# A Mamba-style scan with a routed expert layer: three of sixteen state sums moved from VectorE to ScalarE and GpSimd, and a rearranged end

## The chip, the cores and the metric

The kernel runs on one core of a Trainium2 chip. Its time is the device time in microseconds (us) from launch to the last store. The kernel before took 1439.51 us (median of three runs, 1438.04 to 1442.42).

Engines are named as the profile names them: PE is the matrix engine, DVE the vector engine, ACT the scalar (activation) engine, POOL is GpSimd, and SP issues most of the transfers. Every engine works through its own list of instructions strictly in order and waits on semaphores.

## What is computed

All numbers are fp32. There are 32 sequences of 256 tokens with 128 features.

```python
x = x + mamba(layernorm(x), ...)
x = x + moe(layernorm(x), ...)

# mamba: 256 channels, 16 states for each channel
h = conv1d(xc, conv_w) + conv_b; u = h.T
dt = clip(sigmoid(u @ dt_w.T + dt_b), 1e-4, 1.0)
dA = exp(clip(dt * A)); dB = dt * B * u
state = dA * state + dB + 1e-6             # over time
y = sum over the 16 states of state * C, + D * u
y = (y * silu(z)) @ out_w.T

# moe: 8 experts of 256 hidden units, the best two for each token, and a shared one
shared = silu(x @ sg.T) * (x @ su.T) @ sd.T
routed = w0 * expert_a(x) + w1 * expert_b(x)
out = shared + routed
```

## The kernel before

**Groups and states.** The tokens are cut into 16 groups of 512 (two sequences). For each group the 16 states are taken one after another, so a *unit* is one state of one group, and there are 256. One unit passes through four engines:

1. ACT computes the decays `dA` (`decays`, L727 to L741) and for 5 of the 16 states also the inputs `dBT` by token (`state_input`, L784); POOL computes `dBT` for the other 11 (L621). `KINDS` says which.
2. PE transposes `dBT` into the two banks `p_db`, one for each half of the channels (`inputs_by_channel`, L854, names `i0`, `i1`).
3. DVE scans over time, `h <- dA, p_db`, one instruction for each half (L1070, names `s0`, `s1`).
4. PE transposes `h` back into `p_hT`, two banks (`states_by_token`, L866, name `h`), and DVE multiplies by C and adds to `yT` (`sum_states`, L1073, names `y0`, `y1`): four instructions of 128x256. For state 0 they are plain products (L1086), for the others product and sum (L1088).

`p_db` and `p_hT` exist once: PE can't write the next state before DVE has read the one there. `h` and `yT` exist twice.

**Around the states.** While the states of group g run, PE also computes group g+1's convolution, dt, B, C and z (names `xnT`, `u0`, `u1`, `dt0`, `dt1`, `bc`, `z0`, `z1`, `wT0`, `wT1`), all through one bank `p_misc`. For group g-1 come the transposes of `yT` (`yb0`, `yb1`), the skip term on DVE (`yd0`, `yd1`, L1101), the gate on POOL (L651), the output projection (`op`), the residual (`x1`, L1095), the second layer norm, and the router.

**Experts.** Two groups form a routed batch, and the last two groups are batches of their own. DVE sorts the tokens by expert in 29 small steps (`route`, L1112), the last of which writes `expert_of` (L1193). POOL scatters the rows to DRAM by indirect transfers (L665). Then come quads of four 128-row tiles: SP loads each tile's expert weights (384 KB) into a ring of eight (L514), PE computes gate, up and down (`G`, `U`, `N`), ACT the silu, DVE the product (`P`, L1199). POOL gathers the two results of each token back (L679), and DVE adds them, weighted, in eight instructions for a group (`add_routed`, L1206, name `C`). Every quad uses the same two banks `p_gu`, so its gate waits for the product of the quad before.

**What sets the order.** Tables of names, one line for each of the 16 units of a group (`PE_SLOTS`, `DVE_SLOTS`, `ACT_SLOTS`, `POOL_SLOTS`, `SP_SLOTS`), say in which order an engine does what; a line is called a slot here. `x` is a decay, `d` a state input, `c` a clamp, `S` scatters and gathers. `plan()` gives each piece of the expert layer a slot number, and lags from it. Nothing is reordered at run time.

## Time and profile before

| | before |
|---|---|
| median of 3 runs | 1439.51 us |
| profiled execution | 1441.34 us, span 1439.6 us |
| PE busy | 1240.6 us, 86% |
| DVE busy | 1221.1 us, 85% |
| ACT busy | 893.8 us, 62% |
| POOL busy | 791.7 us, 55% |
| chain that ended last | DVE 38%, PE 33%, issue 13%, ACT 9%, POOL 4% |

The span falls into three parts. Until 44.9 us constants and weights are loaded, and the first group is prepared. From 44.9 us, when the first scan starts, to about 1304 us the 256 units run. After that the last group's output, its router, and the remaining expert tiles follow, until 1439.6 us. In the middle part PE and DVE are both busy about nine tenths of the time, so a share of the span alone doesn't tell which of them sets the pace at a given place; the prediction reads stretches of one group instead.

### The profile page before, as it was taken

The page shows a single profiled execution, that of the slowest core. Times are in us where ns is not written, and L with a number is a line of the kernel's source. Part 1 is how long each engine was busy: PE and PEld are TensorE (multiplying, and loading weights), DVE is VectorE, ACT ScalarE, POOL GpSimd, SP SyncE. Part 2 cuts the span into 40 slices and gives each one's busy share as a digit, 9 for nine tenths or more (in the row PEclk, how much of TensorE's full clock was granted, in tenths as well). Part 3 has the DMA queues.
Part 4 walks back from the last instruction along what each step waited for, and adds up shares of the span by engine and source line. Part 5 has one row for each costly group of instructions (what it writes and reads, how often), then busy time and mean ns, then how long its engine had stood idle before and what let it go on. Part 6 is the DMA issues. An engine that isn't in the chain of part 4 may idle for free.

```text
span 1439.6 us, 27184 instructions
## 1 busy us (share of the span) xinstructions
PE 1240.6 (86%) x8709; PEld 1023.9 (71%) x8709; DVE 1221.1 (85%) x2396; ACT 893.8 (62%) x1399; POOL 791.7 (55%) x1318
## 2 busy tenths in 40 slices
PE   6788897899889898998989898998989898887883
PEld 3566666587777787786768777777777677776873
DVE  0699999898898989899998989999898989995331
ACT  2774757476776766666865766766765757752221
POOL 3445453854377553856467553866557553773342
PEclk9799999999999999999999999999999999998997
DMA  5000000032324143133423142133324142246873
GB/s 173 1 1 8 2 8 5 30 115 63 107 84 127 39 127 114 54 98 96 118 80 125 39 133 90 59 118 96 118 71 132 34 132 63 77 144 184 263 234 114
DMA packets 110655, 132.30 MB, mean 92 GB/s; under 512 B 10032, under 2 KB 81584, under 8 KB 110384
## 3 DMA queue, kind: packets, MB, share of 16 engines
q1 hardware_dynamic: 102320, 113.73, 25.6%
q0 software_dynamic: 8192, 16.79, 4.0%
q8 instruction: 73, 1.20, 0.3%
q14 instruction: 70, 0.57, 0.1%
HBM read 102.37 MB, written 28.11 MB: 91 GB/s over the span
## 4 chain that ended last, share of the span: by engine, by line
DVE 38%; PE 33%; issue 13%; ACT 9%; POOL 4%; DMA 2%; DVEq 0%; SPq 0%; POOLq 0%; ACTq 0%
DVE h L1070 17%; DVE yT L1088 12%; PE p_misc L908 6%; PE p_hT L876 5%; PE p_db L862 4%; PE p_dn L1015 4%; PE p_gu L1003 3%; PE p_misc L919 3%; ACT dA L740 2%; PE p_misc L902 2%; PE p_gu L995 2%; PE p_misc L945 1%; DVE x L1216 1%; POOL ysel L679 1%; POOL xs_dram L665 1%
## 5 line engine op out<-in xcount | busy, mean ns | idle before, releaser
L1070 DVE TENSOR_TENSOR_SCAN h<-dA,p_db 128x512 f32<-128x512 f32 x512 | 598.8, 1203 | 76.4 <-PE p_db L862 49.0
L632 POOL TENSOR_SCALAR dBT<-wT,bcT 128x256 f32<-128x256 f32 x704 | 338.6, 481 | 373.0 <-ACT wT L769 204.8
L1088 DVE SCALAR_TENSOR_TENSOR yT<-p_hT,bcT,yT 128x256 f32<-128x256 f32 x960 | 396.9, 471 | 9.4 <-PE p_hT L876 9.4
L862 PE MATMUL p_db<-ident,dBT 128*128 128x128 f32 x2048 | 297.3, 278 | 82.8 <-DVE h L1070 70.0
L862 PEld LDWEIGHTS p_db<-ident,dBT 128*128 128x128 f32 x2048 | 233.8, 142 | 145.6 <-issue 121.3
L740 ACT ACTIVATE dA<-dt_sb,A_sb 128x510 f32<-128x510 f32 x512 | 329.7, 709 | 5.4 <-DVE h L1070 4.7
L876 PE MATMUL p_hT<-ident,h 128*128 128x128 f32 x2048 | 292.7, 280 | 25.7 <-DVE yT L1088 16.5
L876 PEld LDWEIGHTS p_hT<-ident,h 128*128 128x128 f32 x2048 | 231.6, 143 | 68.4 <-DVE yT L1088 36.6
L679 POOL DMA_INDIRECT ysel<-ys_dram,slot x128 | 123.4, 964 | 97.3 <-DVE x L1216 38.4
L795 ACT ACTIVATE dBT<-wT,eps,bcT 128x256 f32<-128x256 f32 x320 | 163.5, 587 | 7.6 <-PE p_db L862 7.6
L665 POOL DMA_INDIRECT xs_dram<-xn,slot x128 | 126.8, 990 | 56.6 <-issue 36.0
L1199 DVE TENSOR_TENSOR hm<-p_gu,hm 128x512 f32<-128x512 f32 (+1 forms) x132 | 87.0, 663 | 71.7 <-PE p_gu L1003 70.6
L812 ACT ACTIVATE hm<-p_gu 128x512 f32<-128x512 f32 (+1 forms) x132 | 72.1, 581 | 109.3 <-PE p_gu L995 106.5
L1015 PE MATMUL p_dn<-wring,hm 128*128 128x128 f32 x764 | 106.3, 287 | 12.5 <-DVE hm L1199 12.5
L908 PE MATMUL p_misc<-xnT,wtap 128*128 128x512 f32 x256 | 116.1, 595 | 0.8 <-ACT u_sb L751 0.8
L1015 PEld LDWEIGHTS p_dn<-wring,hm 128*128 128x128 f32 x764 | 97.3, 201 | 15.4 <-DVE hm L1199 5.8
L1003 PE MATMUL p_gu<-xT,wring 128*128 128x128 f32 x764 | 105.6, 286 | 1.2 <-ACT hm L812 1.2
L1003 PEld LDWEIGHTS p_gu<-xT,wring 128*128 128x128 f32 x764 | 99.0, 202 | 10.1 <-issue 8.2
L995 PE MATMUL p_gu<-xT,wring 128*128 128x128 f32 x764 | 100.7, 276 | 6.0 <-issue 5.7
L751 ACT ACTIVATE u_sb<-p_misc,chan_sb 128x512 f32<-128x512 f32 x32 | 21.8, 680 | 127.8 <-PE p_misc L908 127.8
L995 PEld LDWEIGHTS p_gu<-xT,wring 128*128 128x128 f32 x764 | 93.2, 192 | 10.0 <-issue 7.7
L812 ACT ACT_TABLE_LOAD x53 | 68.0, 1283 | 34.1 <-PE p_gu L995 33.6
(115 smaller groups left out, 1374.3 us busy)
## 6 DMA issues: line engine op xcount, KB each, us to landing
wring<-w_moe_dram SPq DMA_DIRECT2D x191, 384.0 KB, 4.3
xt<-xs_dram SPq DMA_DIRECT2D x41, 256.0 KB, 4.8
ys_dram<-yo SPq DMA_DIRECT2D x41, 256.0 KB, 2.3
x_sb<-x_dram SPq DMA_DIRECT2D x16, 256.0 KB, 4.3
out_dram<-x SPq DMA_DIRECT2D x16, 256.0 KB, 2.6
xs_dram<-ysel SPq DMA_DIRECT2D x4, 512.0 KB, 5.5
xs_dram<-xn,slot POOLq DMA_INDIRECT x128, 2.3
ysel<-ys_dram,slot POOLq DMA_INDIRECT x128
```

Source lines behind the costliest of these rows:

```text
L632: op = pool.tensor_scalar(dBT[:, j % DBT_RING, c], wT[:, g % 2, c], bcT[:, g % 2, c, n:n + 1], STATE_EPS, ALU.mult, ALU.add)
L665: pool.indirect_dma_start(out=xs[b % 2], out_offset=bass.IndirectOffsetOnAxis(ap=slot[:, b % ROUTE_RING, j, c:c + 1], axis=0), in_=xn2[:, ...
L740: act.activation(dst[:, :, 1:], src[:, :, 1:], ACT.Exp, scale=A_sb[:, half, n:n + 1]).then_inc(exp_done, 1)
L795: op = act.activation(dBT[:, j % DBT_RING, c], wT[:, g % 2, c], ACT.Identity, scale=bcT[:, g % 2, c, n:n + 1], bias=eps[:])
L862: mm = pe.transpose(p_db[half][:, c * P:(c + 1) * P], dBT[:, j % DBT_RING, c, half * P:(half + 1) * P], ident[:])
L876: mm = pe.transpose(p_hT[pair][:, c, half * P:(half + 1) * P], h[:, j % 2, half, t0:t0 + P], ident[:])
L908: mm = pe.matmul(p_misc[:].rearrange("p (s t) -> p s t", s=SPG), wtap[:, t, half * P:(half + 1) * P], xnT[:, :, t:t + SEQ], start=t == 0, ...
L995: mm = pe.matmul(p_gu[i][:, half, cols], w[:, half * P:(half + 1) * P], tokens, start=True, stop=True)
L1003: mm = pe.matmul(p_gu[i][:, half, cols], w[:, HID + half * P:HID + (half + 1) * P], tokens, start=True, stop=True)
L1015: mm = pe.matmul(p_dn[:, t], hm[:, i, half, t % 2 * P:(t % 2 + 1) * P], w[:, 2 * HID + half * DM:2 * HID + (half + 1) * DM], start=half == ...
L1070: dve.tensor_tensor_scan(h[:, j % 2, half], dA[:, j % DA_RING, half], p_db[half][:], 0.0, ALU.mult, ALU.add).then_inc(scan_done, 1)
L1088: op = dve.scalar_tensor_tensor(yT[:, g % 2, cc], p_hT[pair][:, c], scalar, yT[:, g % 2, cc], ALU.mult, ALU.add)
```

## The change

- **The sums of states 0, 1 and 2 of each group leave DVE.** ACT multiplies the transposed state by C (`multiply_state`, names `m0`, `m1`): state 0 into `yT`, states 1 and 2 into a new buffer `y_more` that exists once. POOL adds `y_more` to `yT` (`add_more`). DVE's sum of state 3 waits for POOL's last addition. PE's transposes of a state wait for `mul_done` where ACT reads the one before.
- **The routed rows of groups 0 to 11 are added by POOL**: one product of 128x1024 and two additions of 128x512 (`add_routed` on POOL). DVE keeps groups 12 to 15.
- **At the end there are three sets of banks for the quads** (`p_gu`, `p_db`, `p_hT`, with `hm` and the two halves of `wT` as their buffers), and eight more places for expert weights in `dA`, free once the last scan is done. Quads come one slot apart from slot 257, two apart from slot 236.
- **New order tables**, with decays four units ahead in place of three, clamps two in place of one, rings of five in place of three for the router's results. The last three batches scatter two chunks in a slot.

The core of the diff:

```diff
+BY_ACT = 3
+COMB_DVE = 4
-CLAMP_LEAD = 1
-EXP_LEAD = 3
+CLAMP_LEAD = 2
+EXP_LEAD = 4
-ROUTE_RING = 3
+ROUTE_RING = 5
 DVE_SLOTS = (
-    "stats1 s0 s1 y0 y1", "P Q s0 C s1 y0 y1 yd0 P Q", "s0 s1 yd1 Q y0 y1 C", "s0 s1 C y0 y1 C P Q P",
+    "s0 s1 y0 y1", "stats1 P s0 s1 y0 C y1 Q yd0 P Q s0 Q", "s1 yd1 y0 y1 C", "C s0 s1 y0 y1 P C Q P",
...
-LAST_SCATTER = 6
+LAST_SCATTER = 3
-FAST_SLOTS = 12
-FAST_FROM = NS * GROUPS - FAST_SLOTS
-FAST_QUAD = 2
+TAIL = NS * GROUPS + 1
+TAIL_QUAD = 1
+TAIL_WEIGHT = 3
+END_SLOTS = 20
+END_FROM = NS * GROUPS - END_SLOTS
+END_QUAD = 2
-WEIGHT_LEAD = 2
+WEIGHT_LEAD = 1
+def bank_sets():
+    sets, before, last = [], [], {}
+    for at, (slot, _) in enumerate(ORDER):
+        chosen = 0 if slot < TAIL else (sets[-1] + 1) % 3
...
+        gu_banks = [p_gu, [p_db[i][:].rearrange("p (f t) -> p f t", f=2) for i in range(2)], p_hT]
+        hm_of = [hm[:]] + [wT[:, j].rearrange("p (i f) t -> p i f t", f=2) for j in range(2)]
...
+            def add_more(g, n, pair):
+                if g is None:
+                    return
+                pool.wait_ge(mul_done, sums_before(NS * g + n, pair, True))
+                at_least(pool, more_added, PAIRS * ((BY_ACT - 1) * g + n - 2) + pair + 1 if n > 1 else 0)
+                chunks = slice(2 * pair, 2 * pair + 2)
+                pool.tensor_tensor(yT[:, g % 2, chunks], yT[:, g % 2, chunks], y_more[:, chunks], ALU.add
+                                   ).then_inc(more_added, 1)
...
+            def add_routed(g, j):
+                b, m = place_of(g)
+                if j == 0:
+                    pool.wait_ge(ysel_loaded, 128 * (g + 1))
+                    pool.wait_ge(dn_emptied, QUAD["shared", g] + 1)
+                    shares = weight[:, b % ROUTE_RING, :, CHUNKS * m:CHUNKS * (m + 1)]
+                    pool.tensor_tensor(ysel[:], ysel[:], shares.rearrange("p j (c o) -> p j c o", o=1).broadcast_to(
+                        [P, 2, CHUNKS, DM]), ALU.mult).then_inc(comb_scaled, 1)
+                    pool.wait_ge(comb_scaled, g + 1)
+                else:
+                    pool.wait_ge(comb_done, 2 * g + 1)
+                pool.tensor_tensor(x1[:, g % X1_RING], x1[:, g % X1_RING], ysel[:, j], ALU.add).then_inc(comb_done, 1)
...
+            def multiply_state(g, n, pair):
+                j = NS * g + n
+                act.wait_ge(hT_in_psum, PAIRS * j + pair + 1)
...
+                for c in range(2):
+                    cc = 2 * pair + c
+                    into = yT[:, g % 2, cc] if n == 0 else y_more[:, cc]
+                    op = act.activation(into, p_hT[pair][:, c], ACT.Copy, scale=bcT[:, g % 2, cc, NS + n:NS + n + 1])
+                op.then_inc(mul_done, 1)
...
                 g, n = divmod(j, NS)
+                if n < BY_ACT:
+                    return
                 dve.wait_ge(hT_in_psum, PAIRS * j + pair + 1)
+                if n == BY_ACT == 1:
+                    dve.wait_ge(mul_done, sums_before(j - 1, pair, True))
+                elif n == BY_ACT:
+                    dve.wait_ge(more_added, PAIRS * ((BY_ACT - 1) * (g + 1) - 1) + pair + 1)
```

**ACT at the start of a group.** The decays of states 4 and on (`dA`), the inputs of states 3 and 4 (`dBT` x8), a quad's silu (`hm`), and the transposed input (`xnT`). Before:

```order
L740 ACTIVATE dA<-dt_sb,A_sb 128x2x255 x6
L795 ACTIVATE dBT<-wT,eps,bcT 128x256 x8
L740 ACTIVATE dA<-dt_sb,A_sb 128x2x255 x2
L812 ACT_TABLE_LOAD
L812 ACTIVATE hm<-p_gu 128x512
L812 ACTIVATE hm<-p_gu 128x2x128
L747 ACTIVATE xnT<-p_misc 128x2x256
L820 ACTIVATE yo<-p_dn 128x512
L740 ACT_TABLE_LOAD
L740 ACTIVATE dA<-dt_sb,A_sb 128x2x255 x2
L795 ACTIVATE dBT<-wT,eps,bcT 128x256 x4
```

The same place of the changed kernel:

```order
L835 ACTIVATE dA<-dt_sb,A_sb 128x2x255 x6
L891 ACTIVATE dBT<-wT,eps,bcT 128x256 x8
L911 ACTIVATE yT<-p_hT,bcT 128x256 x4
L835 ACTIVATE dA<-dt_sb,A_sb 128x2x255 x2
L931 ACT_TABLE_LOAD
L931 ACTIVATE hm<-p_gu 128x512
L931 ACTIVATE hm<-p_gu 128x2x128
L842 ACTIVATE xnT<-p_misc 128x2x256
L911 ACTIVATE y_more<-p_hT,bcT 128x256 x4
L939 ACTIVATE yo<-p_dn 128x512
L891 ACTIVATE dBT<-wT,eps,bcT 128x256 x4
L835 ACT_TABLE_LOAD
```

The three groups of four products (the third follows two rows later) stand between work that was there before; nothing was taken away between them.

**DVE at the start of a group.** `stats` is the first layer norm of the next group, `h` the scans, `yz` the skip term, `hm` the product of a quad. Before, from just ahead of state 0's scans to state 3's:

```order
L1047 BN_STATS stats<-x_sb 128x6 x4
L1050 BN_AGGR mv<-stats 128x2 x4
L1070 SCALAR_TENSOR_TENSOR h<-dA,p_db 128x512 x2
L1088 SCALAR_TENSOR_TENSOR yT<-p_hT,bcT,yT 128x256 x4
L1199 TENSOR_TENSOR hm<-p_gu,hm 128x512
L1070 SCALAR_TENSOR_TENSOR h<-dA,p_db 128x512 x2
L1086 TENSOR_SCALAR yT<-p_hT,bcT 128x256 x4
L1101 SCALAR_TENSOR_TENSOR yz<-u_sb,chan_sb,p_misc 128x512
L1070 SCALAR_TENSOR_TENSOR h<-dA,p_db 128x512 x2
L1101 SCALAR_TENSOR_TENSOR yz<-u_sb,chan_sb,p_misc 128x512
L1088 SCALAR_TENSOR_TENSOR yT<-p_hT,bcT,yT 128x256 x4
L1070 SCALAR_TENSOR_TENSOR h<-dA,p_db 128x512 x2
```

The same place of the changed kernel, on to state 4's scans:

```order
L1201 SCALAR_TENSOR_TENSOR h<-dA,p_db 128x512 x2
L1219 SCALAR_TENSOR_TENSOR yT<-p_hT,bcT,yT 128x256 x4
L1178 BN_STATS stats<-x_sb 128x6 x4
L1181 BN_AGGR mv<-stats 128x2 x4
L1332 TENSOR_TENSOR hm<-p_gu,hm 128x512
L1201 SCALAR_TENSOR_TENSOR h<-dA,p_db 128x512 x2
L1233 SCALAR_TENSOR_TENSOR yz<-u_sb,chan_sb,p_misc 128x512
L1201 SCALAR_TENSOR_TENSOR h<-dA,p_db 128x512 x2
L1233 SCALAR_TENSOR_TENSOR yz<-u_sb,chan_sb,p_misc 128x512
L1201 SCALAR_TENSOR_TENSOR h<-dA,p_db 128x512 x2
L1332 TENSOR_TENSOR hm<-p_gu,hm 128x512
L1201 SCALAR_TENSOR_TENSOR h<-dA,p_db 128x512
```

The statistics now follow state 0's scans, and no sum stands between the scans of states 1, 2 and 3. The sum that follows first is state 3's, between the two halves of state 4's scan.

**POOL at the start of a group whose batch is being scattered.** Changed kernel only: scatters (`xs_dram`), the layer norm (`rs`, `xn`), the gate (`yz`), and the additions.

```order
L635 TENSOR_TENSOR rs<-rs,neg_half 128x4
L638 TENSOR_SCALAR xn<-x_sb,nm,rs 128x128 x4
L726 TENSOR_TENSOR yz<-yz,sz 128x512
...
L740 DMA xs_dram<-xn,slot 2944x128 x2
L708 TENSOR_TENSOR yT<-yT,y_more 128x512 x2
L698 TENSOR_SCALAR dBT<-wT,bcT 128x256 x4
L740 DMA xs_dram<-xn,slot 2944x128 x2
...
L726 TENSOR_TENSOR yz<-yz,sz 128x512
L708 TENSOR_TENSOR yT<-yT,y_more 128x512 x2
```

The four additions stand behind scatters, a layer norm and both gates in the same queue.

## Rows read from the trace of the kernel before

**Rows 1.** The page's part 1: busy time, share, instructions.

```profile
PE 1240.6 (86%) x8709; PEld 1023.9 (71%) x8709; DVE 1221.1 (85%) x2396; ACT 893.8 (62%) x1399; POOL 791.7 (55%) x1318
```

**Rows 2.** Timeline of DVE (start, duration, instructions): state 0's sums, two groups apart.

```profile
658.87 1.63 DVE L1086 TENSOR_SCALAR yT<-p_hT,bcT 128x256 f32<-128x256 f32 x4
...
822.67 1.63 DVE L1086 TENSOR_SCALAR yT<-p_hT,bcT 128x256 f32<-128x256 f32 x4
```

**Rows 3.** Busy time by stretch: length, each engine (instructions), PE clock, DMA share, GB/s.

```profile
380.00:1180.00 800.00, 722.13 (x5235) 600.58 (x5234) 742.09 (x1446) 550.43 (x855) 484.15 (x773) 1.00 0.30 92
816.06:835.33 19.27, 17.59 (x116) 14.15 (x115) 17.73 (x30) 14.89 (x26) 15.87 (x24) 0.94 0.33 92
835.33:863.90 28.57, 27.42 (x199) 22.92 (x197) 25.22 (x52) 17.20 (x24) 14.03 (x28) 1.00 0.41 129
863.90:899.40 35.50, 30.67 (x253) 26.19 (x251) 34.07 (x76) 23.52 (x39) 12.49 (x21) 1.00 0.29 88
```

**Rows 4.** Timeline of DVE around the start of the group at 816 us.

```profile
811.25 2.31 DVE L1216 SCALAR_TENSOR_TENSOR x<-ysel,weight,x 128x128 f32<-128x128 f32 x8
...
814.86 0.87 DVE L1047 BATCH_NORM_STATS2 stats<-x_sb 128x6 f32<-128x128 f32 x4
...
816.06 2.30 DVE L1070 TENSOR_TENSOR_SCAN h<-dA,p_db 128x512 f32<-128x512 f32 x2
...
837.57 1.63 DVE L1088 SCALAR_TENSOR_TENSOR yT<-p_hT,bcT,yT 128x256 f32<-128x256 f32 x4
```

**Rows 5.** Timeline of PE: transposes of state 3 and of state 4.

```profile
836.20 1.04 PE L876 MATMUL p_hT<-ident,h 128*128 128x128 f32 x8
...
841.60 1.04 PE L876 MATMUL p_hT<-ident,h 128*128 128x128 f32 x8
```

**Rows 6.** Timeline of ACT in the same group (last number in brackets: idle before).

```profile
817.41 4.03 ACT L795 ACTIVATE dBT<-wT,eps,bcT 128x256 f32<-128x256 f32 x8
821.35 1.31 ACT L740 ACTIVATE dA<-dt_sb,A_sb 128x510 f32<-128x510 f32 x2
824.49 1.28 ACT L812 ACT_TABLE_LOAD   x1 [1.82 <-PE p_gu L995]
...
851.98 1.09 ACT L812 ACTIVATE hm<-p_gu 128x512 f32<-128x512 f32 x2
```

**Rows 7.** Groups of instructions by line (busy, mean ns | idle before, releaser).

```profile
L764 ACT ACTIVATE bcT<-p_misc 128x128 f32<-128x128 f32 x16 | 4.3, 266 | 14.4 <-PE p_misc L945 14.4
...
L651 POOL TENSOR_TENSOR yz<-yz,sz 128x512 f32<-128x512 f32 x32 | 40.9, 1278 | 34.5 <-DVE yz L1101 34.3
```

**Rows 8.** Timeline of POOL: a layer norm's ends, the inputs ahead of a batch's scatters.

```profile
843.13 0.20 POOL L566 TENSOR_SCALAR rs<-mv 128x4 f32<-128x4 f32 x1 [5.33 <-DVE mv L1050]
...
844.87 1.74 POOL L572 TENSOR_SCALAR xn<-x,nm,rs 128x128 f32<-128x128 f32 x4
...
891.82 4.38 POOL L632 TENSOR_SCALAR dBT<-wT,bcT 128x256 f32<-128x256 f32 x8 [18.45 <-ACT wT L769]
```

**Rows 9.** Timelines of POOL and DVE at one moment of the router.

```profile
870.87 2.50 POOL L646 TENSOR_TENSOR w_sb<-dt_sb,u_sb 128x512 f32<-128x512 f32 x2
```

```profile
872.30 1.15 DVE L1140 TENSOR_TENSOR key<-rest,top 128x64 f32<-128x64 f32 x1
```

**Rows 10.** Timeline of the end, DVE: the last scans, the last router step.

```profile
1301.60 2.31 DVE L1070 TENSOR_TENSOR_SCAN h<-dA,p_db 128x512 f32<-128x512 f32 x2
...
1347.01 0.17 DVE L1193 TENSOR_SCALAR expert_of<-expert_f 1x15 int32<-1x15 f32 x1
```

**Rows 11.** Timeline of the end, POOL: gathers of groups 12, 13 and 15.

```profile
1360.51 0.99 POOL L679 DMA_INDIRECT ysel<-ys_dram,slot  x1 [3.19 <-issue]
...
1377.81 0.95 POOL L679 DMA_INDIRECT ysel<-ys_dram,slot  x1 [7.49 <-DVE x L1216]
...
1423.09 0.95 POOL L679 DMA_INDIRECT ysel<-ys_dram,slot  x1 [18.77 <-DMA ys_dram<-yo]
...
1431.88 0.95 POOL L679 DMA_INDIRECT ysel<-ys_dram,slot  x1 [0.30 <-issue]
```

More of the change, by code:

```diff
@@ L34 @@
 DT_MIN = 1e-4
-BATCHES = tuple((g, g + 1) for g in range(0, GROUPS - 2, 2)) + ((GROUPS - 2,), (GROUPS - 1,))
+ALONE = 2
+BATCHES = tuple((g, g + 1) for g in range(0, GROUPS - ALONE, 2)) + tuple((g,) for g in range(GROUPS - ALONE, GROUPS))
 MOST = max(len(gs) for gs in BATCHES) * CHUNKS
@@ L177 @@
 QUAD = {quad: at for at, (_, quad) in enumerate(ORDER)}
+def bank_sets():
+    sets, before, last = [], [], {}
+    for at, (slot, _) in enumerate(ORDER):
+        chosen = 0 if slot < TAIL else (sets[-1] + 1) % 3
+        sets.append(chosen)
+        before.append(last.get(chosen))
+        last[chosen] = at
+    return sets, before
+BANK_SET, BEFORE = bank_sets()
 def tiles_of_quad(quad):
@@ L217, in plan @@
         slot = max(ended[b] + GATHER_LAG, last_gather)
-        per = 1 if ended[b] < FAST_FROM else 4
+        per = 1 if ended[b] < TAIL else 4
         for g in gs:
@@ L296, in routed_quad, with sums_before @@
     return b, at - XT0[b]
+def sums_before(j, pair, by_act):
+    if j < 0:
+        return 0
+    full, n = divmod(j, NS)
+    if by_act:
+        return PAIRS * (full * BY_ACT + min(n, BY_ACT)) + (pair + 1 if n < BY_ACT else 0)
+    return PAIRS * (full * (NS - BY_ACT) + max(0, n - BY_ACT)) + (pair + 1 if n >= BY_ACT else 0)
 def of_kind(kind, j):
@@ L450, in build @@
         mac_done = sem("mac_done")
+        mul_done = sem("mul_done")
+        more_added = sem("more_added")
         yz_ready = sem("yz_ready")
@@ L461, in build @@
         w_loaded = [sem(f"w_loaded{j}") for j in range(W_RING)]
+        spare_loaded = [sem(f"spare_loaded{j}") for j in range(SPARE)]
         gate_in_psum = sem("gate_in_psum")
@@ L704, in _ @@
                         weigh_u(ahead, int(name[1]))
+                    if name in ("m0", "m1") and u - NS * k < BY_ACT - 1:
+                        add_more(group_of(k, 0), u - NS * k + 1, int(name[1]))
                     if name in ("gate0", "gate1") and behind is not None:
                         gate(behind, int(name[4]))
+                    if name == "C":
+                        for g, j in due.get(("comb", u), ()):
+                            if g < GROUPS - COMB_DVE:
+                                add_routed(g, j)
                     if name == "S":
@@ L807, in silu @@
                 at = QUAD[quad]
-                at_least(act, down_in_psum, at)
+                into, banks = hm_of[BANK_SET[at]], gu_banks[BANK_SET[at]]
+                if BEFORE[at] is not None:
+                    act.wait_ge(down_in_psum, BEFORE[at] + 1)
+                elif BANK_SET[at]:
+                    act.wait_ge(scan_done, HALVES * UNITS)
                 for i in range(2):
@@ L811, in silu @@
                     act.wait_ge(gate_in_psum, 2 * at + i + 1)
-                    act.activation(hm[:, i, :, 0:n], p_gu[i][:, :, 0:n], ACT.Silu).then_inc(silu_done, 1)
+                    act.activation(into[:, i, :, 0:n], banks[i][:, :, 0:n], ACT.Silu).then_inc(silu_done, 1)
             def empty_down(b, q):
@@ L827, in _ @@
                         state_input(u + DB_LEAD)
+                    if name in ("m0", "m1") and u - NS * k < BY_ACT:
+                        multiply_state(group_of(k, 0), u - NS * k, int(name[1]))
                     if name in MISC_STAGE and group_of(k, MISC_STAGE[name]) is not None:
@@ L871, in states_by_token @@
                 for pair in range(PAIRS):
-                    at_least(pe, mac_done, PAIRS * (j - 1) + pair + 1)
+                    if j and (j - 1) % NS < BY_ACT:
+                        pe.wait_ge(mul_done, sums_before(j - 1, pair, True))
+                    elif j:
+                        pe.wait_ge(mac_done, sums_before(j - 1, pair, False))
                     for c in range(2):
```

140 lines of the change are left out of this document (87 added, 53 removed), and 28 rows, old and new, of tables (ACT_SLOTS, DVE_LAST, DVE_SLOTS, PE_SLOTS).

## Prediction

> **What bounds the kernel now.** I read the busy shares first: PE 86%, DVE 85%, ACT 62%, POOL 55% [rows 1]. They name two candidates and settle nothing. In the timeline of DVE the reader looks for a landmark that comes once in a group, state 0's sums. They are 163.8 us apart over two groups (658.87 to 822.67), so 81.9 us for a group [rows 2]. Over 800 us of that, PE is busy 722.1 and DVE 742.1, which makes 73.9 and 76.0 us in a group, with 8.0 and 5.9 us idle [rows 3]. Neither can be the bound alone; the next view has to say where each one is.
>
> I cut the group that starts at 816.06 us into three stretches [rows 3].
> - A, the scans of states 0 to 3: 19.3 us, PE busy 17.6, DVE 17.7.
> - B, states 4 to 8, where the convolution, dt and B, C of the next group lie on PE: 28.6 us, PE busy 27.4, DVE 25.2. PE sets the pace.
> - C, states 9 to 15: 35.5 us, DVE busy 34.1, PE 30.7. DVE sets the pace.
>
> The sums that the change takes from DVE all lie in A. B is PE's and C keeps all its own. That is the main reading: what is removed is large, and where it is removed, something else is nearly as late.
>
> **Stretch C and its edge: what comes off.** Four sums take 1.63 us [rows 2]; end to end that is 0.39 each, so twelve make 4.7 us for a group. They are in A. In C two things go. The statistics of the next layer norm stood ahead of state 0's scans and now follow them: from 814.86 to 816.06, 1.2 us for every group [rows 4]. The eight routed additions, 2.3 us [rows 4], are in C in one group of two; in the other they lie in B, under PE, and I count them at nothing. That gives 1.2 + 2.3/2 = 2.35 us for a group.
>
> **Stretch A: what takes the sums' place.** The path was scan, transposes, sum on DVE. It is now scan, transposes, product on ACT, addition on POOL, sum of state 3 on DVE. I follow ACT's list from the start of state 0's scans (time 0). The third pair of decays waits for those scans, 2.3 us [rows 4], and takes 1.3, so 3.6. Eight state inputs take 4.0 [rows 6]: 7.6. Then come state 0's four products.
>
> No row shows such a product (128x256 from a PSUM bank, with a scale for each partition). From below, a plain copy of 128x128 from PSUM takes 0.27 us [rows 7]; from above, a state input of the same size, with scale and bias, is 4.03/8 = 0.50 end to end [rows 6]. The nearest is the state input, less its bias. I take 0.40, so 1.6 for a state; the ends give 1.1 and 2.0.
>
> Onward: 9.2 after state 0; decays 1.3, 10.5; table load 1.3 and two silus 1.1 [rows 6], 12.9; the transposed input 0.5, 13.4; state 1's products, 15.0; a state input 2.0 and an output of a quad 0.6, 17.6; table load and decays 2.6, 20.2; state 2's products, 21.8. Before, PE finished transposing state 3 at about 837.1, 21.0 us after the start [rows 5]. Now these transposes wait for state 2's products and end near 22.5, because nothing was taken out of ACT's list between them.
>
> POOL is second in the path. A two-input operation of 128x512 takes 1.28 us [rows 7], so the four additions are 5.1 us for a group, on an engine that is busy 15.9 of 19.3 us in A [rows 3]. A batch's scatters can begin when the next states' inputs are out, at 896.2 [rows 8]; that is 4.4 us before the next group's time 0, which is 1.2 us of statistics behind the end of C. Up to the last addition the new order has ten scatters (1.26 each, as the gathers, 1423.09 to 1431.88 for seven [rows 11]), two state inputs (2.2 each), a layer norm (3.5) [rows 8], two gates (2.6) and the four additions (5.1): 28.2 us. I get the last addition out at 24 to 25, so state 3's sums end near 27, where they ended at 839.2 (23.1) before [rows 4]. PE's transposes of state 4 were reached at 841.60, 25.5 us after the start [rows 5], because PE was late anyhow. So 2.4 us of the delay are hidden and 1 to 1.5 us are not. I take a loss of 1.0 us for a group; from zero, if ACT and POOL run ahead of this, up to 5.1, if one more block of routed additions stands in front.
>
> Main part: 2.35 - 1.0 = 1.35 us for each of 13 groups with expert work, 17.6 us. For the first three I take nothing: they have no quads, and the 2.3 us of decays and the state inputs stand before the products just as well.
>
> **Two rules of the Trainium skill.** The router step at 872.30 took 1.15 us, while POOL's products of two SBUF inputs ran from 870.87 to 873.37; it ended with them [rows 9]. The sums, of which one input is a PSUM bank, take 1.63 us for four in every row here [rows 2, 4]. The Trainium skill (SBUF — State Buffer, "Who interferes with whom") says that a DVE instruction with two SBUF inputs and a GpSimd instruction that reads SBUF exclude each other, and that one with at most one SBUF input doesn't contend. The trace agrees. By that rule the additions cost DVE nothing. It speaks against the change in one place: the two products `w0` and `w1` now stand in two slots of the router, and each may stop a step for some 0.9 us, 8 us in all over eight routed batches.
>
> For ACT's product the Trainium skill (ScalarE: Activation LUTs, "What ACT_TABLE_LOAD costs") gives 280 ns and 0.833 ns for each element, an estimate of 0.49 us for 256 elements. The trace's end-to-end times are below its figure. With 0.49 state 2's products would be out 1.1 us later, and the main part would save about 14 us less.
>
> **The end.** Time from the last scan to the last router step, 1303.9 to 1347.2: 43.3 us [rows 10]. In it stand 2.3 us of routed additions and waits for quads behind one another; with more banks and group 11's rows on POOL I take 3 us off. Then: eight scatters, 10.2 us; idle 3.2; four groups of eight gathers, 10.05 each; idle between them 7.5, about as much again, and 18.8; and 1432.83 to 1439.6 for the last landing, the additions and the store [rows 11]. The gathers need nothing from the banks but that batch 8's quads are done. The 18.8 us were that wait. With three sets of banks and sixteen places for weights it shrinks to what the others show, 7.5, and the 3.2 go to 0.5. That is 14 us, with the 3 us 17. POOL's list of 40 indirect transfers at 1.26 us then holds the end, and no bank helps further.
>
> The last group gets two more quads and scatters at double rate; I set this at nothing, within 4 us either way.
>
> **The sum.** 1441.3 (the profiled execution) - 17.6 - 17 = 1406.7. The median of the runs is 1.8 us lower, so 1405 us. The difference that a measurement can tell from none is 0.3%, 4.3 us.
>
> **Rivals.**
> 1. The sums come off in full, since the tables also move PE's work. For it: DVE has 5.9 us idle in a group, and half of PE's 8.0 may be DVE's doing. Against: A, where the sums are, has both engines at 17.7 of 19.3, and B is PE's. DVE loses 4.7 + 2.3 = 7.0 us; PE's 73.9 and 2 us of unavoidable gaps stop it at 76, so 5.9 x 13 + 4.7 x 3 = 91 us, and 17 at the end: 1332. Half of it: 1377.
> 2. Slower: the chain over ACT and POOL takes DVE's place. State 3's sum waits for POOL's fourth addition, and everything behind it waits too. If the loss in A is 5.1 us in place of 1.0 (one block of routed additions, 2.6 + 2 x 1.28, ahead of it), the main part costs 2.75 x 13 = 36 us more, less 17: 1458. It decides from a loss of 2.35 + 17/13 = 3.7 us on. For it: ACT's list is full there, and POOL's too. Against: before, 2.4 us were spare.
> 3. The end gives nothing, because the expert weights of batch 8 land no earlier (the wait of 18.8 us stays). Then the main part alone: 1439.5 - 17.6 = 1422.
>
> **How the numbers follow.** Forecast 50%, rival 1 in full or in part 25%, rival 2 13%, rival 3 12%. The forecast's own range is 1385 to 1425. For eight in ten I reach down past the half of rival 1, to 1362, and up to where rival 2 has just lost the whole gain, 1437. Faster by over 0.3%: the forecast, rivals 1 and 3, less some edge, 85%; within 0.3% 5%; slower 10%.
>
> **What would show it.** In the changed profile the landmark, now state 3's sums, should lie about 161 us apart for two groups (between 159 and 163); at 152 rival 1 is right, above 164 rival 2. DVE's busy time should fall by 16 x 4.7 + 12 x 2.3, about 100 us, much more than the span does. Its idle time before state 3's sums should name POOL's additions. ACT's products should have some 0.4 us end to end. At the end the idle time before group 15's gathers should be near 7 us. The forecast is wrong if stretch A is shorter than 18 us, or if PE waits for `mul_done` less than 0.5 us a group.

## The result: 3% slower, and the profile after

The changed kernel takes 1484.83 us (median of four runs, 1483.70 to 1484.93), the kernel before, beside it, 1438.78 (1437.89 to 1442.42). The ratio is 1.030, 95% interval 1.028 to 1.032. Forecast were 1405 us, within 1362 to 1437. It went the way of rival 2, with more than its price.

Busy times of the changed kernel's page stand against [rows 1]: DVE lost 83 us of work (forecast were about 100; part of the difference is in the router, see below), PE 7, ACT gained 70 and POOL 136. The span rose by 43.5.

```profile
PE 1233.4 (83%) x8709; PEld 1026.0 (69%) x8709; DVE 1138.5 (77%) x2108; ACT 963.9 (65%) x1592; POOL 927.7 (63%) x1418
```

The landmark is the first layer norm's statistics, once in a group, in DVE's timeline. Two groups of the changed kernel are 170.45 us apart, against 163.8 in [rows 2].

```profile
763.85 0.85 DVE L1178 BATCH_NORM_STATS2 stats<-x_sb 128x6 f32<-128x128 f32 x4
...
934.30 0.85 DVE L1178 BATCH_NORM_STATS2 stats<-x_sb 128x6 f32<-128x128 f32 x4
```

The same stretches as in [rows 3], of the changed kernel: 800 us, then A, B, C of a group, then A of the next.

```profile
380.00:1180.00 800.00, 697.17 (x5072) 586.50 (x5072) 665.46 (x1213) 572.90 (x933) 550.07 (x804) 0.99 0.29 87
...
840.02:864.22 24.20, 18.27 (x128) 14.63 (x128) 14.31 (x25) 21.23 (x41) 19.78 (x27) 1.00 0.68 204
864.22:893.53 29.31, 27.48 (x201) 23.18 (x201) 23.37 (x44) 17.55 (x25) 19.11 (x30) 1.00 0.28 84
893.53:930.50 36.97, 31.37 (x245) 28.04 (x244) 35.98 (x75) 24.99 (x40) 16.31 (x26) 0.91 0.22 65
930.50:952.50 22.00, 18.26 (x128) 14.62 (x128) 14.32 (x26) 20.89 (x41) 17.90 (x26) 1.00 0.34 103
```

A grew from 19.3 to 24.2 us. DVE is busy only 14.3 of them, PE 18.3: PE's idle time in A went from 1.7 to 5.9, DVE's from 1.5 to 9.9. Neither is the bound there; both wait for ACT and POOL, and for each other. B grew by 0.7 us (even groups) and 1.1 (odd ones); C grew by 0.2 in the even groups and fell by 3.4 in the odd ones. DVE's timeline shows where A is lost:

```profile
840.02 2.32 DVE L1201 TENSOR_TENSOR_SCAN h<-dA,p_db 128x512 f32<-128x512 f32 x2
...
848.45 2.33 DVE L1201 TENSOR_TENSOR_SCAN h<-dA,p_db 128x512 f32<-128x512 f32 x2
856.96 0.75 DVE L1233 SCALAR_TENSOR_TENSOR yz<-u_sb,chan_sb,p_misc 128x512 f32<-128x512 f32 x1 [6.18 <-PE p_misc L1011]
857.62 2.32 DVE L1201 TENSOR_TENSOR_SCAN h<-dA,p_db 128x512 f32<-128x512 f32 x2
863.62 0.69 DVE L1332 TENSOR_TENSOR hm<-p_gu,hm 128x512 f32<-128x512 f32 x1 [3.67 <-PE p_gu L1134]
864.22 1.21 DVE L1201 TENSOR_TENSOR_SCAN h<-dA,p_db 128x512 f32<-128x512 f32 x1
```

The first wait, 6.18 us, is for `yb1`, which the new PE table has behind `xnT`, the transposes of the normalized input. In the whole profile such waits are 75.9 us; before they were 1.3. ACT and POOL in the same moments:

```profile
847.54 1.53 ACT L911 ACTIVATE yT<-p_hT,bcT 128x256 f32<-128x256 f32 x4
...
855.12 0.60 ACT L931 ACTIVATE hm<-p_gu 128x512 f32<-128x512 f32 x1 [2.91 <-PE p_gu L1125]
855.62 0.59 ACT L842 ACTIVATE xnT<-p_misc 128x512 f32<-128x512 f32 x1
856.09 1.57 ACT L911 ACTIVATE y_more<-p_hT,bcT 128x256 f32<-128x256 f32 x4
...
862.65 1.55 ACT L911 ACTIVATE y_more<-p_hT,bcT 128x256 f32<-128x256 f32 x4
```

```profile
850.80 1.75 POOL L638 TENSOR_SCALAR xn<-x_sb,nm,rs 128x128 f32<-128x128 f32 x4
...
865.54 2.50 POOL L708 TENSOR_TENSOR yT<-yT,y_more 128x512 f32<-128x512 f32 x2
```

The loop is to be read here. POOL's layer norm is out at 852.55, 12.5 us after the start of A (before: 824.83, 8.8 us). PE's transposes of it start at 852.69, a gate matmul (L1125) stands behind them, ACT's silu waits for that gate and ends at 855.72, and state 1's products begin at 856.09, though PE had finished transposing that state at 851.3. Four products take 1.53 us, 0.38 each: the 0.40 taken was right.

PE's list shows how the delays pass on. Its waits between 400 and 1180 us add up to 68 us before and 97 in the changed kernel, about 3 us more for a group, which is what a group lost. None of these lines has a counterpart before:

```profile
PE p_misc L1011 <- ACT xnT L842: 9.5, 9, 1.2
PE p_misc L1011 <- DVE yT L1219: 9.0, 9, 1.0
...
PE p_misc L1021 <- POOL xn L638: 5.5, 4, 1.4
...
PE p_hT L1000 <- ACT y_more L911: 1.5, 9, 0.2
```

The last of them is the wait of the transposes for products themselves (`mul_done`), under 0.2 us for a group. The prediction had named less than 0.5 us there as a sign against itself. The products act through what stands behind them, and hardly through that wait.

Cut at the scans in DVE's timeline, the loss of 61.4 us up to the last scan (1301.60 before, 1362.98 after) is: first scan 4.1 later; groups 0 to 3, 1.9; groups 4 to 13, 30.7; groups 14 and 15, 24.7. Behind the last scan 17.9 us came back (138.0 before, 120.1 after). Windows of group 15 (A, B) and of the time behind the last scan, changed kernel:

```profile
1273.40:1305.00 31.60, 19.19 (x129) 17.59 (x128) 14.74 (x20) 23.78 (x44) 23.95 (x27) 0.89 0.36 111
1305.00:1327.20 22.20, 19.43 (x171) 18.43 (x170) 22.13 (x44) 10.51 (x15) 15.48 (x28) 1.00 0.33 108
...
1365.30:1483.10 117.80, 76.28 (x579) 70.75 (x577) 37.74 (x107) 25.21 (x47) 55.83 (x60) 0.89 0.59 187
```

The gathers of the last four groups in POOL's timeline, to be laid beside [rows 11]: the longest gap ahead of one is 9.0 us, where it was 18.8.

```profile
1432.60 0.94 POOL L754 DMA_INDIRECT ysel<-ys_dram,slot  x1 [5.72 <-DVE x L1350]
...
1451.28 0.94 POOL L754 DMA_INDIRECT ysel<-ys_dram,slot  x1 [9.01 <-DVE x L1350]
...
1466.49 0.94 POOL L754 DMA_INDIRECT ysel<-ys_dram,slot  x1 [5.51 <-DMA ys_dram<-yo]
```

### The profile page after: what moved, and what is told of

The parts are those of the page before. It is cut to its first block, busy times and chain, and to the rows that moved or that the text cites. A ratio compares the mean times of both kernels' runs of the same rounds, so it can differ in the third digit from the quotient of the medians.

```text
span 1483.1 us, 27197 instructions
## 1 busy us (share of the span) xinstructions
PE 1233.4 (83%) x8709; PEld 1026.0 (69%) x8709; DVE 1138.5 (77%) x2108; ACT 963.9 (65%) x1592; POOL 927.7 (63%) x1418
## 3 DMA queue, kind: packets, MB, share of 16 engines
q1 hardware_dynamic: 102320, 113.73, 24.7%
## 4 chain that ended last, share of the span: by engine, by line
PE 33%; DVE 23%; issue 15%; ACT 13%; POOL 13%; DMA 1%; SPq 1%; POOLq 0%; DVEq 0%; ACTq 0%
DVE h L1201 11%; DVE yT L1219 8%; PE p_db L983 5%; PE p_hT L1000 5%; PE p_dn L1146 4%; PE p_misc L1032 4%; POOL dBT L698 3%; ACT dA L835 3%; PE p_gu L1125 3%; PE p_gu L1134 3%; PE p_misc L1043 2%; POOL xs_dram L740 2%; POOL ysel L754 2%; PE p_misc L1026 2%; ACT dBT L891 2%
## 5 line engine op out<-in xcount | busy, mean ns | idle before, releaser
L1219 DVE SCALAR_TENSOR_TENSOR yT<-p_hT,bcT,yT 128x256 f32<-128x256 f32 x832 | 344.5, 470 | 29.8 <-PE p_hT L1000 15.3
L983 PE MATMUL p_db<-ident,dBT 128*128 128x128 f32 x2048 | 302.7, 280 | 75.0 <-DVE h L1201 64.9
L835 ACT ACTIVATE dA<-dt_sb,A_sb 128x510 f32<-128x510 f32 x512 | 332.5, 712 | 22.6 <-DVE h L1201 20.6
L983 PEld LDWEIGHTS p_db<-ident,dBT 128*128 128x128 f32 x2048 | 239.6, 144 | 138.7 <-issue 108.2
L1000 PEld LDWEIGHTS p_hT<-ident,h 128*128 128x128 f32 x2048 | 235.5, 144 | 66.4 <-issue 41.3
L740 POOL DMA_INDIRECT xs_dram<-xn,slot x128 | 127.3, 994 | 58.4 <-issue 34.3
L1332 DVE TENSOR_TENSOR hm<-p_gu,hm 128x512 f32<-128x512 f32 x118 | 77.6, 663 | 63.5 <-PE p_gu L1134 63.3
L931 ACT ACTIVATE hm<-p_gu 128x512 f32<-128x512 f32 x118 | 65.3, 584 | 72.9 <-PE p_gu L1125 67.9
L708 POOL TENSOR_TENSOR yT<-yT,y_more 128x512 f32<-128x512 f32 x64 | 80.0, 1271 | 29.8 <-ACT y_more L911 29.7
L1146 PE MATMUL p_dn<-wring,hm 128*128 128x128 f32 x664 | 91.4, 284 | 5.2 <-DVE hm L1332 4.2
L1125 PE MATMUL p_gu<-xT,wring 128*128 128x128 f32 x664 | 87.1, 277 | 2.4 <-ACT xT L877 1.2
L1134 PE MATMUL p_gu<-xT,wring 128*128 128x128 f32 x664 | 88.3, 278 | 0.3 <-ACT hm L931 0.3
L1146 PEld LDWEIGHTS p_dn<-wring,hm 128*128 128x128 f32 x664 | 83.8, 199 | 6.6 <-issue 2.5
L931 ACT ACT_TABLE_LOAD x54 | 69.3, 1283 | 24.8 <-PE p_gu L1125 21.9
```

Source lines behind the costliest of these rows:

```text
L740: pool.indirect_dma_start(out=xs[b % 2], out_offset=bass.IndirectOffsetOnAxis(ap=slot[:, b % ROUTE_RING, j, c:c + 1], axis=0), in_=xn2[:, ...
L835: act.activation(dst[:, :, 1:], src[:, :, 1:], ACT.Exp, scale=A_sb[:, half, n:n + 1]).then_inc(exp_done, 1)
L931: act.activation(into[:, i, :, 0:n], banks[i][:, :, 0:n], ACT.Silu).then_inc(silu_done, 1)
L983: mm = pe.transpose(p_db[half][:, c * P:(c + 1) * P], dBT[:, j % DBT_RING, c, half * P:(half + 1) * P], ident[:])
L1000: mm = pe.transpose(p_hT[pair][:, c, half * P:(half + 1) * P], h[:, j % 2, half, t0:t0 + P], ident[:])
L1146: mm = pe.matmul(p_dn[:, t], hm_of[BANK_SET[at]][:, i, half, t % 2 * P:(t % 2 + 1) * P], w[:, 2 * HID + half * DM:2 * HID + (half + 1) * D ...
```

## Experiments

The runs came in five groups, each on a chip of its own with runs of the kernel before beside it. That took 1465 us on four of these chips and 1441 on the fifth. Two steady groups of the changed kernel's lists take 170.2 to 170.4 us on four chips; with the lists of before they take 163.8 on the first chip and 164.1 to 164.9 on two others, so a difference of 1 us to before is no more than their scatter. The end differs more. So two numbers are given: the ratio to before on the same chip, and the length of two steady groups (start of group 6's scans to start of group 14's, over four, from DVE's timeline), with A of an even and an odd group. These are to be laid beside 163.8 (19.3, 19.0) before and 170.3 (24.2, 22.0) after.

**The changed kernel once more.** No edit.

> The changed kernel as it is, once more, beside the others of this group, since the end of the program takes another time from chip to chip. The steady groups should be those of its first profile to 0.1 us (stretch A 24.2 and 22.0 us, two groups 170.5); its ratio to the kernel before was 1.030 and is expected between 1.03 and 1.045.

1.0436 (1.041 to 1.046); two groups 170.4 us, A 24.2 and 22.0. The steady loss repeats. From the last scan to the end it takes 154.9 us here, 120.1 on the first chip. With the old lists (experiment 10, banks alone) that stretch takes 146.6 us on another of the chips with 1465 us: the gain of 17.9 us behind the last scan is seen on the first chip only.

**1. yb1 early.**

```
-    "h i0 i1 G U N", "h X xnT i0 i1 U N G yb1"
+    "h i0 i1 G U N yb1", "h X xnT i0 i1 U N G"
```

> One move in the changed kernel: PE transposes the second half of yT (yb1) at the end of slot 1, ahead of the layer norm's transposes (xnT), as in the kernel before, and not at the end of slot 2. Theory P (the place of yb1): DVE's 75.9 us of waits for this transpose are the loss, since the scan of state 3 is queued behind it. It expects stretch A (scan of state 0 to scan of state 4) to fall from 24.2 and 22.0 us to about 20 and the time to 1440 us, the gain of the tail (some 16 us) just paying the rest. Theory L (the lists of ACT and POOL): the transposes xnT wait for a late layer norm of POOL, the silu of ACT waits for the gate matmul behind xnT, the products m0, m1 stand behind that silu, and PE's transposes of h wait for the products. It expects that the wait of DVE only moves from yb1 to p_db or p_hT: A stays within 1 us of before, 1470 to 1485 us.

1.0444 (1.042 to 1.047), two groups 170.8, A 24.2 and 22.6. Waits of DVE between 400 and 1180 us, first in the changed kernel, then here:

```profile
DVE yz L1233 <- PE p_misc L1011: 44.6, 9, 6.2
DVE hm L1332 <- PE p_gu L1134: 36.2, 17, 3.7
DVE h L1201 <- PE p_db L983: 27.0, 27, 2.1
```

```profile
DVE hm L1332 <- PE p_gu L1134: 66.5, 17, 7.4
DVE h L1201 <- PE p_db L983: 36.8, 32, 2.2
...
DVE yz L1233 <- PE p_misc L1011: 1.5, 9, 0.3
```

43 us of one wait turned into 40 us of two others. The longest wait in the list was worth nothing by itself. Theory P falls, L stands so far.

**2. All sums back on DVE,** in the changed order (`BY_ACT = 0`).

> The changed kernel with its own order, but the sums of all sixteen states on DVE: no products on ACT, no additions of them on POOL. Theory L expects A to fall to 20 us in spite of 4.7 us more work of DVE in it, since PE waits no more for products and additions: 3 us in each of 13 groups, about 1445 us. Theory P expects A to stay at 22 to 24 (yb1 still stands behind xnT), or to grow by what DVE has to do behind it: 1485 to 1530 us. If the chain of products were harmless, the time must rise by up to 4.7 x 16 = 75 us.

1.054 (1.051 to 1.057), two groups 172.8, A 26.8 and 24.8. L's expectation did not come true: without the products A is longer still, as theory P had it. Neither theory holds in both runs.

**3. Both together.** The edit of 1 and that of 2.

> The changed kernel's order with all sums on DVE, as in the run before with sums on DVE, and yb1 ahead of xnT too, so that DVE's sum of state 1 no longer stands behind the wait for yb1. That run alone had A of 25.8 and 25.8 us, yb1 alone 24.2 and 22.6. If the two waits cover for each other, A falls to 21 to 22.5 us, two groups to 166 to 168. If only the late layer norm and the longer list of PE set A, it stays at 24 to 26.

1.0208 (1.018 to 1.023), two groups 166.3, A 22.8 and 22.1. The two waits cover for each other. With yb1 late the products cost nothing, and even save 2.5 us (170.3 with, 172.8 without); with yb1 early they cost 4.5 us (170.8 with, 166.3 without). Of the 6.5 us that two groups lost, 2.5 stay with the new order, in which the routed rows are still on POOL.

**4. One state's products.** As 3, with `BY_ACT = 1`: state 0 on ACT, nothing on POOL.

> The changed kernel with yb1 ahead of xnT and the product of state 0 alone on ACT. With no state on ACT two groups took 166.3 us, with three 170.7. If the cost goes with the number of products: 167.5 to 168. If it comes with the second and third (PE's transposes wait for products that stand behind the silu, state 3's sum for POOL): 165 to 166.5.

1.0172 (1.015 to 1.020), two groups 164.6, A 22.4 and 20.8, and so 1.7 us less than with none. It is the second and third state that cost: 6.2 us for two groups. Only they need `y_more`, a free place in it, and POOL's additions. No run separates ACT's eight further products from these additions.

**5. Products in the old lists.** The kernel before, with `BY_ACT = 3` and

```
-ACT  "x V E d d X",       "x V d xnT E",       "x V E X"
+ACT  "x m0 m1 V E d d X", "x m0 m1 V d xnT E", "m0 m1 x V E X"
-POOL "gate0 c d S c",       "S gate1 d c c"
+POOL "gate0 m0 m1 c d S c", "m0 m1 S gate1 d c c"
```

> The kernel before with one part of the change: the products of states 0 to 2 on ACT and two additions of each pair on POOL, put into the old lists where the sums' transposes are out (ACT slots 1 to 3 ahead of the silu, POOL slots 2 and 3). Everything else, the routed rows, the order of the rest and the end too, is that of before. Theory O (the new order of the lists, not the moved work, stretches A): A stays at 19.3 and 19.0 us or falls by up to 1 us, and the time is 0.990 to 1.003 of before. Theory M (the moved work itself, a chain of ACT and POOL in the recurrence): A grows to 21 to 23 us as in the changed kernel, 1.02 to 1.035.

1.0393 (1.036 to 1.042), two groups 172.1: M in kind, and more in the time than it said. But A, at 20.3 and 21.3, lies under or at the low end of M's range, and more was lost in B, which grew from 28.6 and 26.7 to 30.0 and 30.1. From PE's waits, 400 to 1180 us:

```profile
PE p_misc L1030 <- ACT xnT L840: 14.8, 9, 2.1
PE p_hT L998 <- DVE yT L1224: 13.4, 17, 1.9
PE p_misc L1024 <- POOL yz L724: 8.2, 5, 1.7
PE p_misc L1036 <- POOL xn L636: 7.4, 5, 1.5
```

The convolution waits for ACT's copy `xnT`, queued behind products; the output projection waits for POOL's gate, queued behind additions. The second layer norm's transposes wait for POOL too. None of the three waits of 14.8, 8.2 and 7.4 us is in PE's list of before, whose smallest entry is 0.3 us; the fourth is 11.7 there. In these lists the moved work costs by what is queued behind it.

**6. One state in the old lists.**

> The kernel before with the product of state 0 alone on ACT (in ACT's slot 1, ahead of the silu), nothing on POOL; DVE's sum of state 1 then adds to it. It tells ACT's share of the cost from POOL's. With three states on the old lists two groups took 172 to 173 us instead of 164.7. If every product costs on ACT's list (1.6 us in front of the state inputs and the silu, which PE waits for), one state costs about a third, 2.5 to 3 us in two groups, ratio 1.010 to 1.015. If the additions on POOL and the wait of DVE and PE for them are the cost, one state costs nothing or gains DVE's 1.6 us: two groups 162 to 165 us, 0.99 to 1.001.

0.998 (0.9963 to 0.9997), two groups 165.3, on another chip 164.9 with the lists of before. The only version under 1, by 0.2%: one state's products are free, and hardly a gain either. That DVE is not alone in setting A is the likely reason. Against 172.1 with three states, the second and third cost 6.8 us in two groups, much as the 6.2 in the new order.

**7. Routed rows, from both sides.** First the changed kernel with all rows on DVE (`COMB_DVE = 16`), then the kernel before with rows on POOL (`COMB_DVE = 4`, `C` in POOL's table).

> The changed kernel with the additions of the routed rows of all sixteen groups on DVE (COMB_DVE 16), so that POOL has 4.5 us less in each of twelve groups. Theory R (POOL's routed additions and gathers hold up the layer norm, and with it PE's transposes): A of the groups that follow such a block falls from 24.2 to about 22.0, 2.2 us in six groups, and DVE's 2.3 us for each group cost something in stretch C: 1475 to 1490 us. Without R nothing is won in A and DVE's 12 x 2.3 = 28 us come on top: 1500 to 1512 us.

> The kernel before with the routed rows of the first twelve groups added on POOL, in its old lists (POOL's additions at the slots of the changed kernel), and nothing else. In the changed order this was worth 0.9 us in two groups: 2.1 off stretch C of the odd groups, 1.2 more in A of the even ones. Expected from that: ratio 0.990 to 0.998. If POOL's 4.5 us hold up the layer norm in the old order more than DVE gains, 1.000 to 1.01.

1.0438 (1.041 to 1.047) with two groups at 171.2, and 1.0099 (1.008 to 1.012) with 166.9. In the changed order A of the even groups fell to 23.0, half of what theory R said, and C of the odd ones grew by 2.1: the rows on POOL are worth 0.9 us in two groups there, and the whole time does not show it. The second run missed its first range and came out in the second. In the old lists C of the odd groups is 2.2 us shorter (33.7 to 31.5), A of the even ones 4.8 longer (24.1). The 4.5 us of additions and the gathers stand ahead of state 2's input on POOL, and PE waits for it. PE's wait in A of group 10, then its windows before, during and after:

```profile
PE p_db L981 <- POOL dBT L696: 3.9, 1, 3.9
```

```profile
826.60:832.30 5.70, 1.72 (x12) 1.26 (x13) 5.69 (x10) 5.63 (x11) 4.73 (x7) 0.84 0.46 131
832.30:837.40 5.10, 5.10 (x24) 5.10 (x25) 2.33 (x2) 1.28 (x1) 4.61 (x9) 0.51 0.01 3
837.40:842.00 4.60, 4.56 (x42) 4.32 (x40) 3.95 (x7) 1.84 (x4) 3.68 (x4) 1.00 0.17 45
```

After 3.9 us idle PE goes on at a granted clock of 0.51, the level of 1.2 GHz, for 5 us, which costs another 2.5, an estimate from half the speed over these 5 us. Why the same rows are a gain of 0.9 in the changed kernel is not shown; that its chain of products is as late anyway would explain it.

**8. Both on the kernel before.**

> Both of these on the kernel before: routed rows on POOL and the product of state 0 on ACT. If the two save DVE's time independently, the sum of both differences; if each only uncovers PE, no more than the better one.

1.0066 (1.004 to 1.009). With 0.998 and 1.0099 alone, the sum would be 1.008, which lies in the interval; the better one alone does not. The two are independent within the noise.

**9. Four moves against PE's waits.** yb1 early (PE), `stats1` ahead of `s0` (DVE), `ln1` ahead of gathers (POOL), `m0 m1` ahead of `V` (ACT).

> The changed kernel with four moves that aim at PE's waits in A: yb1 back ahead of xnT (PE), the statistics of the layer norm back ahead of state 0's scans (DVE), the layer norm ahead of two gathers (POOL), state 1's products ahead of the silu that waits for a gate matmul behind xnT (ACT). PE was idle 5.9 and 3.7 us of A, before 1.7 and 2.6. Theory O: these waits are the loss, A falls by 2.5 to 4 us, two groups from 170.5 to 164 to 167 us, and the ratio to the changed kernel is 0.970 to 0.985. If the loss is not in these waits (theory M: PE's transposes of h wait for products and additions wherever they stand), two groups stay within 1.5 us of 170.5.

> The changed order with all sums on DVE and yb1 ahead of xnT (1.0208 of before, two groups 166.3 us, before 163.8), and besides the statistics of the layer norm back ahead of state 0's scans and the layer norm ahead of two gathers on POOL. Theory N (the remaining 2.5 us of two groups are the late layer norm): two groups 163.5 to 165 us, ratio 1.008 to 1.015. If they are PE's longer list in A (one more expert matmul block there), it stays within 0.7 us of 166.3.

1.0428 (1.040 to 1.045), two groups 170.7; and the same moves with the sums on DVE 1.0294 (1.026 to 1.033), 167.2. In the first, A fell to 20.9 in odd groups and stayed at 24.2 in even ones on average, and C got the 1.2 us of statistics back. The time is within what theory M said. With the sums on DVE A fell by 0.8 and 1.2, C grew by as much, and B of the odd groups by 0.6: theory N falls. The late layer norm is not the remaining cost; which of the new list's moves is stays open.

**10. The end.** The kernel before with the changed end; that with batch 6's scatters spread; the changed kernel with them spread; the kernel before with three sets of banks alone.

```
-    put("scatter", scatter_from(b) + c // chunks_per_slot(b), b, c)
+    put("scatter", scatter_from(b) + ((0, 1, 2, 3, 4, 4, 5, 5)[c] if b == 6 else c // chunks_per_slot(b)), b, c)
```

> The kernel before in its main part (its lists for the sixteen groups, its leads, all sums and all additions on DVE), with the end of the changed one: its lists for the last stages, three sets of banks and sixteen places for weights, the quads at double pace for the last twenty slots, two chunks of scatters in a slot from batch 6 on. From the last residual to the end the changed kernel takes 101.5 us, before 117.4: that expects 1439 - 16 = 1423 us. If the double rate of batch 6's scatters is what stretches group 15's A from 17.7 to 31.6 us, that group is longer here too, by 5 to 14 us, and the time is 1428 to 1437 us. If the tail's gain hangs on the additions that POOL took over, about 1439 us.

> The kernel before with the end of the changed one, as in the run with the tail alone (1.0167 of before; A of group 15 34.3 us), with the same spreading of batch 6's scatters. Theory S: A of group 15 falls from 34.3 to 20 to 25 us, the ratio from 1.0167 to 1.005 to 1.010. If the 16 us that the tail of the changed kernel saved in its first profile hold on this chip, it would be under 1.

> The changed kernel with one edit: the eight chunks of scatters of batch 6 are spread over six slots (0,1,2,3,4,4,5,5 behind the first) and not over four, while the quads keep their slots. Theory S (scatters at double rate stand on POOL ahead of the inputs of states 2 and 3 of group 15, and PE, ACT and DVE wait behind them): group 15's A, 34.5 us on the chip of the last runs and 31.6 in the first profile, falls to 22 to 27 us, and the time by 7 to 12 us. If the group waits for something else (the shared experts' quad, weights), A stays and the time is that of the changed kernel, 1.0436 of before, within 3 us.

> The kernel before with all its lists, rates and numbers, and only three sets of banks and the sixteen places for weights behind the last scan. Theory W (the resources themselves shorten the end): the waits of the gate matmuls for products and of the weight loads for free places go, 5 to 15 us less, ratio 0.990 to 0.997. Theory T (only the quicker pace of the changed lists uses them): within 3 us of before, 0.998 to 1.002.

1.0167 (1.014 to 1.020), 1.0141 (1.011 to 1.018), 1.0512 (1.048 to 1.055), 1.0001 (0.998 to 1.002). The banks and places alone are worth nothing: T. The changed end costs 25 us, and 22 with the scatters spread, where it was expected to save 16. Group 15's A is 34.3 us with the changed end, 19.1 with the old one. Spreading the scatters takes A to 28.6 in the one kernel and from 34.5 to 30.4 in the other, but B of the changed kernel rises from 24.0 to 41.6, as PE's transposes of the rows (`xt`) then wait up to 10.1 us for their transfer. Theory S is half right: the pile of scatters is a part. The doubled pace of quads inside the scans may be another; no run sets it alone.

**11. The old end in the new main part.**

> The changed kernel with the end of the kernel before: its lists for the last stages, two sets of banks and eight places for weights, double pace for the last twelve slots only, one chunk of scatters in a slot for batches 6 and 7. It separates the end's share of the loss from the steady groups'. On this chip the changed kernel is 1.0436 of before, 64 us. Steady groups 4 to 13: 30 us of that. Theory E (the new end costs on this chip, group 15's A 34.5 us against 19.1): A of group 15 is 21 to 24 us, the ratio 1.024 to 1.033. If the end gives its 16 us back as in the first profile, this run is slower than the changed kernel, 1.05.

> The best main part found in the new order (yb1 ahead of xnT, only state 0's product on ACT, routed rows on POOL; two groups 164.6 us, before 164.7) with the end of the kernel before. It starts its scans 4 us later, since POOL's clamps stand ahead of the first inputs, and its groups should be as long as those of before: ratio 1.000 to 1.005, against 1.0172 with the new end. Above 1.010 the end is not what costs there.

1.0658 (1.063 to 1.068) and 1.0373 (1.035 to 1.040): both misses. A of group 15 is indeed 17.2 and 16.6 us, and the last scan of the first starts at 1349.5, 13.5 us earlier than in the changed kernel on the first chip. But behind the last scan both take over 180 us, where before took 138. Both kept the weights' lead of one slot (`WEIGHT_LEAD = 1`, before 2), which is the likely reason: too short for eight places behind the scans. No run changes it alone. PE's largest wait behind 1350 us, in the first:

```profile
PE p_gu L1124 <- DMA wring<-w_moe_dram: 36.4, 10, 5.7
```

So they price the end's cost within the scans, 13.5 us, but not its gain behind them.

## Why the prediction was wrong

- **Stretch C and its edge:** 2.35 us for a group were forecast to come off. Measured (mean of even and odd) 1.6, all of it in the odd groups: 3.4 there, -0.2 in the even ones, where 1.2 were forecast. Right in kind, too large.
- **Stretch A, the failed step.** "2.4 us of the delay are hidden and 1 to 1.5 us are not": a loss of 1.0 was taken, measured are 3.9 (4.9 and 3.0), and 0.9 in B, which was put at nothing. I followed ACT's list as if only its own work filled it and wrote "table load 1.3 and two silus 1.1". The second silu waited 2.91 us for a gate matmul behind `xnT`; up to that wait the list ran as forecast (state 0's products were out at 9.1 us, 9.2 were forecast), and behind it everything was 2.4 to 2.6 us late. State 2's products ended 24.2 us after the start, not 21.8, PE's transposes of state 3 at 26.2, not 22.5, POOL's last addition at 28.0, not 24 to 25, and state 3's sums at 29.6, not 27. And the wait that I named (state 3's sum for POOL's fourth addition) is not where the time shows: DVE waits 6.6 us for it in the whole run. PE's list carries it, where `h` of the next state, `xnT`, `yb1` each wait a little and everything queued behind them moves. I had read the new PE table's `yb1`, but gave it no price. Experiment 9 moved state 1's products ahead of that silu, with three other moves, and two groups stayed at 170.7. So that one wait does not explain the loss by itself: what it gives back is lost elsewhere.

  A wait of the same kind was in the trace of before, where no product stood in the list. The second silu ended 13.4 us after the start there, not at the 12.9 of the forecast, though that had 1.6 us of products ahead of it:

```profile
828.89 0.60 ACT L812 ACTIVATE hm<-p_gu 128x512 f32<-128x512 f32 x1 [2.51 <-PE p_gu L995]
```

- **Rival 2** named the mechanism and its place, if not its size (1458 us against 1485). Its argument against, "before, 2.4 us were spare", held for one state's products (experiment 6), and not for three (experiment 5). State 3's sum waiting for POOL, its own step, is the small part.
- **Rival 1** assumed DVE or PE as the bound of A; PE is busy only 18.3 us of 24.2.
- **The start** was set at nothing: the first scan is 4.1 us later, since POOL's clamps, with a lead of two, wait for more decays ahead of its first inputs. POOL's first inputs start at 45.6 us, where they started at 36.5.
- **The last groups** were set at nothing, within 4 us. They took 24.7 more, of which 13.5 go with the new end by experiment 11, on another chip.
- **The end:** forecast 17 off, measured 17.9 behind the last scan on the first chip. Its parts came out near too: up to the last router step 2.0 off (forecast 3), behind it 15.9 (forecast 14), and the gap ahead of group 15's gathers 5.5 us (forecast 7.5). But the reason given, more banks, is not shown: alone they gave nothing. On the chips with 1465 us the stretch is not shorter at all (154.9 against 146.6). The number is in part luck.

Put into the sum: the main part without start and new end took 61.4 - 4.1 - 13.5 = 43.8 us more, forecast were 17.6 less, which makes a miss of 61.4 (by chance the same figure as the whole loss up to the last scan). So 1406.7 + 61.4 + 4.1 + 13.5 - 0.9 = 1484.8, against 1484.93 for the profiled execution. That the sum closes proves nothing, since its terms are read from the same runs. It says where the miss lies: some 18 us of the 78 are in the start and the new end, which I set at nothing, and most of the rest in A and B.

**The router beside POOL.** The router's steps at 903.88 and 904.78 took 0.86 and 1.19 us while POOL's products of two SBUF inputs ran from 903.39; the second of them takes 0.21 us without a partner (874.95 before).

```profile
903.39 2.50 POOL L721 TENSOR_TENSOR w_sb<-dt_sb,u_sb 128x512 f32<-128x512 f32 x2
```

```profile
903.88 0.86 DVE L1272 TENSOR_TENSOR key<-rest,top 128x64 f32<-128x64 f32 x1
904.78 1.19 DVE L1275 TENSOR_TENSOR key<-key,rank 128x64 f32<-128x64 f32 x1
```

This is what the Trainium skill (SBUF — State Buffer, "Who interferes with whom") says of a DVE instruction with two SBUF inputs beside a reading GpSimd; the trace agrees, 1.6 us for this batch. Before, one such step was stopped already (1.15 us, [rows 9]). Over the whole run the steps `key<-rest,top`, `key<-key,rank` and `rest<-hit,prob` of the seven batches of two groups took 7.4 us more than before, near the 8 us that the prediction gave. Its eight routed batches are nine, seven of two groups and two of one.

The Trainium skill's figure for an activation of 256 elements (ScalarE: Activation LUTs, "What ACT_TABLE_LOAD costs"), an estimate of 0.49 us, is near the 0.46 to 0.48 of a single one in the trace. The same section says that activations back to back overlap by about 93 ns, which makes an estimate of 0.40, the value that the prediction took; the trace has 0.38. So the page did not speak for the slower sum of the prediction.
